# A four-layer graph network: the second layer's update and the output run inside the passes, bucket by bucket

## The reference, cut to what matters

```python
x = x + L0(h)   # edge MLP, summed by dst, then a linear update with a row norm
x = x + L1(h)   # relu(segment_sum(xt[edge_type, dst], src) + bias), xt = h @ weight[r], r = 0..7
x = x + L2(h)   # attention: softmax over the edges of a dst, then a batch norm
x = x + L3(h)   # leaky(segment_sum(w * h[dst], src) @ W + b), w from the degrees by src
```

## Time and profile before

| | us |
|---|---|
| median of 3 runs (5483.92 to 5489.33) | 5488.67 |
| the profiled execution, its own time | 5489.53 |
| its span, first to last instruction | 5487.8 |
| POOL busy | 3830.3 (70%) |
| PE busy | 3680.3 (67%) |
| DVE busy | 3280.8 (60%) |
| ACT busy | 1405.7 (26%) |

### The profile page before, as it was taken

The page is one execution under the profiler, slowest core; times in us unless marked ns, Lnnn a source line. Parts: engine busy times, 40 slices in busy tenths (PEclk is TensorE's granted clock), DMA queues, the critical chain, the costliest instruction groups (busy, mean ns, idle before and its releaser), DMA issues. The chain is left out here.

```text
span 5487.8 us, 118237 instructions
## 1 busy us (share of the span) xinstructions
PE 3680.3 (67%) x13172; PEld 2382.5 (43%) x13177; DVE 3280.8 (60%) x11095; ACT 1405.7 (26%) x4361; POOL 3830.3 (70%) x4005
## 2 busy tenths in 40 slices
PE   5505777777667992666666667777777446676677
PEld 2402443334453441444444456666666324444445
DVE  7315777787643333555555667777777865555556
ACT  0303444444441100000000156655665310000002
POOL 4777777777777776777777537777777257777773
PEclk8755777887788995677777778888888766766768
DMA  2203445444303442445445334444444244445443
GB/s 58 70 26 73 111 111 111 112 111 112 70 3 103 149 144 57 111 112 111 112 111 112 90 92 108 108 108 108 108 109 109 59 112 111 112 111 112 111 111 95
DMA packets 1094230, 543.77 MB, mean 99 GB/s; under 512 B 905511, under 2 KB 991230, under 8 KB 1093881
## 3 DMA queue, kind: packets, MB, share of 16 engines
q0 software_dynamic: 177920, 424.21, 28.0%
q1 hardware_dynamic: 556152, 105.79, 9.7%
q10 hardware_dynamic: 360064, 12.78, 3.6%
HBM read 458.47 MB, written 83.62 MB: 99 GB/s over the span
## 5 line engine op out<-in xcount | busy, mean ns | idle before, releaser
L1311 PE MATMUL psS_plain_src<-got_plain_src,hot_plain_src 128*128 x3328 | 1317.6, 546 | 809.4 <-SPq L1149 562.9
L1311 PEld LDWEIGHTS psS_plain_src<-got_plain_src,hot_plain_src 128*128 128x128 f32 x3328 | 813.8, 266 | 1312.9 <-issue 1189.9
L1194 DVE TENSOR_TENSOR sums<-sums,psS_plain_src 128x257 f32 x1664 | 701.9, 422 | 880.3 <-PE psS_plain_src L1311 718.3
L666 POOL DMA_INDIRECT got_attend_dst<-dram_gtab,recs_attend_dst x832 | 819.6, 985 | 363.3 <-issue 165.6
L542 POOL DMA_INDIRECT dram_rec_src<-rec_src x784 | 766.1, 977 | 289.8 <-issue 241.1
L1166 POOL DMA_INDIRECT got_edge_mlp_dst<-dram_ptab,tile_rec_edge_mlp_dst x784 | 744.3, 949 | 241.8 <-issue 220.1
L1166 POOL DMA_INDIRECT got_plain_src<-dram_htab,tile_rec_plain_src x784 | 743.5, 948 | 242.0 <-issue 219.9
L1166 POOL DMA_INDIRECT got_plain_src<-dram_xtab,tile_rec_plain_src x784 | 743.4, 948 | 241.8 <-issue 214.2
L1322 PE MATMUL psS_edge_mlp_dst<-msg_edge_mlp_dst,hot_edge_mlp_dst 128*128 128x256 f32 x1664 | 653.3, 512 | 151.0 <-DVE sage_sums L1194 123.8
L861 PE MATMUL psS_attend_dst<-msg_attend_dst,hot_attend_dst 128*128 128x264 f32 x1664 | 621.9, 461 | 22.1 <-DVE msg_attend_dst L747 11.9
L1322 PEld LDWEIGHTS psS_edge_mlp_dst<-msg_edge_mlp_dst,hot_edge_mlp_dst 128*128 128x128 f32 x1664 | 344.3, 239 | 290.5 <-DVE sage_sums L1194 105.6
(11 more groups left out here) (347 smaller groups left out, 3957.2 us busy)
## 6 DMA issues: line engine op xcount, KB each, us to landing
dram_xtab<-out_tab SPq DMA_DIRECT2D x48, 1024.0 KB
recs_plain_src<-dram_rec_src ACTq DMA_DIRECT2D x1664, 4.0 KB
tile_rec_plain_src<-dram_rec_src SPq DMA_DIRECT2D x1568, 4.0 KB
recs_edge_mlp_dst<-dram_rec_dst ACTq DMA_DIRECT2D x832, 4.0 KB
recs_attend_dst<-dram_rec_dst SPq DMA_DIRECT2D x832, 4.0 KB
got_attend_dst<-dram_gtab,recs_attend_dst POOLq DMA_INDIRECT x832
dram_rec_src<-rec_src POOLq DMA_INDIRECT x784, 2.1
tile_rec_edge_mlp_dst<-dram_rec_dst SPq DMA_DIRECT2D x784, 4.0 KB
```

The lines of the kernel that those rows point to most:

```text
L666: nc.gpsimd.indirect_dma_start(got[:, u, 0:w], None, table, bass.IndirectOffsetOnAxis(rec_i[:, u, index_word:index_word + 1], 0)).then_inc ...
L1194: nc.vector.tensor_tensor(here, here, psS[t[1] % banks][:, 0:cols], ALU.add).then_inc(added, 1)
L1311: nc.tensor.matmul(psS[t[1] % banks][:, 0:cols], hot[:, t[1], :], flat[:, bass.ds(slots.of(u), cols)], start=True, stop=True).then_inc(sum ...
```

## The change

`run_behind` is a new way to run a ring: from round 5 (`FIRST`) on, after `step(i, u)` it calls `behind(i - 5, u)`. In the two plain passes that is a piece of the work that used to be a stage of its own, on bucket `j = i - 5`, whose sums are complete by then. `RgcnBehind` takes the place of `rgcn_update` and `attention_guard`; `GcnBehind` that of `gcn_output`. Buckets 0 to 46 are done within the rounds, the last two (K = 47 and 48) after the last pair, in `vector_end` and its like, with the range and the guard.

The guard's shift is made from the range alone, with the range in place of the per-node maximum. `c.wide` is kept to the end of the program. It is also set (`c.uneven`) where a bucket `j` of the first 47 has its last pair later than pair `72 + 16 j`, which `PairTables` counts. Where it is set, everything from the pass of L1 on is done again in the old way, on a copy of `x` (`xold`) which SP writes during the pass of L1, one bucket in each round of tiles. `stab` is no longer written on the way that is always taken. The shares in `CUTS` now give 3 rounds of scatters to `place_stage`, then 2, 4, 7, 2, 1 and 10 as before, and 20 to `table_stage` 1.

```diff
-CUTS = 0.04, 0.08, 0.163, 0.306, 0.347, 0.367, 0.57
+CUTS = 0.061, 0.102, 0.184, 0.327, 0.367, 0.388, 0.592
...
+FIRST = 5
...
+    def run_behind(self, eng, step, behind, first, lag):
+
+
+        def a_round(i, more):
+            for u in range(self.size):
+                step(i, u)
+                if more:
+                    behind(i - first, u)
+        a_round(0, False)
+        with eng.Fori(1, first) as i:
+            a_round(i, False)
+        a_round(first, True)
+        with eng.Fori(first + 1, self.rounds - 1) as i:
+            a_round(i, True)
+        a_round(self.rounds - 1, True)
...
+            nc.vector.tensor_tensor(self.late[0:NB, :], self.upto[0:NB, :], c.due[0:NB, :], ALU.is_gt).then_inc(self.lates, 1)
...
+            nc.vector.tensor_scalar(c.uneven[:, :], psX[0:1, 16:17], 0.0, None, ALU.is_gt)
...
+            nc.gpsimd.iota(c.due[:, :], pattern=[[0, 1]], base=U * FIRST - LAG["plain"], channel_multiplier=U,
+                           allow_small_or_imprecise_dtypes=True)
...
+        self.done_by = lambda j: U * (j + FIRST) + 1 - lag
...
+class RgcnBehind(Behind):
+    def keep(self, sp, i):
+        c, rows = self.c, self.c.sh.LAST if isinstance(i, int) and i == self.NB - 1 else P
+        sp.dma_start(c.xold[bass.ds(P * i, rows), :], c.x[0:rows, bass.ds(i, 1), :].rearrange("p a d -> p (a d)")).then_inc(self.kept, 16)
...
+    def vector(self, dve, j, u):
+        nc, c = self.nc, self.c
+        if u == 0:
+            dve.wait_ge(self.added, self.done_by(j))
+            nc.vector.tensor_tensor(self.tmp[:, 0, :], self.row(c.acc, j), c.bias1[:, :], ALU.add).then_inc(self.sums, 1)
+            nc.vector.tensor_copy(self.cnt[:, bass.ds(j, 1)], self.row(c.acc, j, D, D + 1))
+        if u == 1:
+            dve.wait_ge(self.sums, j + 1)
+            dve.wait_ge(self.kept, 16 * (j + 1))
+            x = self.row(c.x, j)
+            nc.vector.scalar_tensor_tensor(x, self.tmp[:, 0, :], 0.0, x, ALU.max, ALU.add).then_inc(self.xs, 1)
+        if u == 2:
+            dve.wait_ge(self.xs, j + 1)
+            self.gate.step()
+            nc.vector.bn_stats(self.stats[:, 0, :], self.row(c.x, j)).then_inc(self.stated, 1)
+            dve.wait_ge(self.stated, 2 * j + 1)
+            self.gate.step()
+            nc.vector.bn_aggr(self.moments[:, 0, :], self.stats[:, 0, :]).then_inc(self.stated, 1)
+            dve.wait_ge(self.stated, 2 * j + 2)
+            nc.vector.tensor_scalar(self.scl[:, 0:1], self.moments[:, 0, 1:2], EPS, None, ALU.add).then_inc(self.begun, 1)
+        if u == 4:
+            dve.wait_ge(self.rooted, j + 1)
+            nc.vector.reciprocal(c.rstd[:, bass.ds(j, 1)], self.scl[:, 0:1]).then_inc(self.scaled, 1)
+            dve.wait_ge(self.scaled, j + 1)
+            nc.vector.scalar_tensor_tensor(c.nbias[:, bass.ds(j, 1)], self.moments[:, 0, 0:1], -1.0, c.rstd[:, bass.ds(j, 1)],
+                                           ALU.mult, ALU.mult).then_inc(self.normed, 1)
+        if u == 15:
+            dve.wait_ge(self.outs, j + 1)
+            self.note(dve, j, 2 * j + 1)
+
+    def note(self, dve, j, zs):
+        nc, c = self.nc, self.c
+        a_src, a_dst = self.row(c.acc, j, D, AW), self.row(c.acc, j, AW, XW)
+        z = self.row(self.z, j, 0, HEADS)
+        dve.wait_ge(self.zs, zs)
+        nc.vector.tensor_tensor(z, a_src, a_dst, ALU.add).then_inc(self.zs, 1)
+        nc.vector.tensor_copy(self.row(c.node, j, 0, HEADS), a_dst)
+        top, low = self.run[:, 0:2 * HEADS], self.run[:, 2 * HEADS:3 * HEADS]
+        nc.vector.tensor_tensor(top, top, self.row(c.acc, j, D, XW), ALU.max)
+        nc.vector.tensor_tensor(low, low, a_src, ALU.min)
+        dve.wait_ge(self.zs, zs + 1)
+        nc.vector.scalar_tensor_tensor(z, z, SLOPE, z, ALU.mult, ALU.max).then_inc(self.zs, 1)
...
+        dve.wait_ge(self.added, self.all)
+        nc.vector.tensor_tensor(self.tmp[:, :, :], c.acc[:, K:NB, 0:D], c.bias1[:, :].unsqueeze(1).to_broadcast([P, 2, D]),
+                                ALU.add).then_inc(self.sums, 1)
...
+        link(all_max(nc, None, dve, self.psR, most, every, 3 * H, self.steps, self.dense, self.diag, c))
+        top = every[:, 0:H].unsqueeze(1).to_broadcast([P, NB, H])
+        nc.vector.tensor_tensor(self.peaks[:, 0, :], every[:, 0:H], every[:, H:2 * H], ALU.add)
+        nc.vector.tensor_copy(self.peaks[:, 1, :], every[:, 0:H])
+        link(nc.vector.tensor_tensor(self.m[:, :, :], c.node[:, 0:NB, 0:H], top, ALU.add))
+        nc.vector.scalar_tensor_tensor(self.peaks[:, :, :], self.peaks[:, :, :], SLOPE, self.peaks[:, :, :], ALU.mult, ALU.max)
+        link(nc.vector.scalar_tensor_tensor(self.m[:, :, :], self.m[:, :, :], SLOPE, self.m[:, :, :], ALU.mult, ALU.max))
+        nc.vector.tensor_tensor(self.z[:, :, :], self.z[:, :, :], self.m[:, :, :], ALU.subtract).then_inc(self.owned, 1)
+        link(nc.vector.tensor_reduce(c.peak[:, :], self.peaks[:, :, :].rearrange("p a h -> p (a h)"), AX.X, ALU.max))
+        nc.vector.tensor_scalar(c.node[:, 0:NB, H:2 * H], self.m[:, :, :], c.peak[:, 0:1], None, ALU.subtract)
+        link(nc.vector.tensor_tensor(self.span[:, :], every[:, 0:H], every[:, 2 * H:3 * H], ALU.add))
+        link(nc.vector.tensor_reduce(self.widest[:, :], self.span[:, :], AX.X, ALU.max))
+        link(nc.vector.tensor_scalar(self.widest[0:1, :], self.widest[0:1, :], SPAN, None, ALU.is_gt))
+        nc.vector.tensor_tensor(c.wide[:, :], self.widest[0:1, :], c.uneven[:, :], ALU.max)
...
+    def scalar(self, act, j, u):
+        nc, c = self.nc, self.c
+        if u == 2:
+            act.wait_ge(self.begun, j + 1)
+            nc.scalar.sqrt(self.scl[:, 0:1], self.scl[:, 0:1]).then_inc(self.rooted, 1)
+        if u == 4:
+            act.wait_ge(self.normed, j + 1)
+            wait_count(act, self.turned, j)
+            nc.scalar.activation(self.h[:, 0, :], self.row(c.x, j), ACT.Relu, bias=c.nbias[:, bass.ds(j, 1)],
+                                 scale=c.rstd[:, bass.ds(j, 1)]).then_inc(self.hs, 1)
+        if u == 6:
+            act.wait_ge(self.turned, j + 1)
+            wait_count(act, self.made, j)
+            nc.scalar.copy(self.hT[:, 0, :], self.psT[:, 0:D]).then_inc(self.hTs, 1)
+        if u == 8:
+            act.wait_ge(self.made, j + 1)
+            nc.scalar.copy(self.row(c.acc, j, 0, XW), self.psO[:, 0:XW]).then_inc(self.outs, 1)
+        if u == 9:
+            act.wait_ge(self.outs, j + 1)
+            act.dma_start(c.gtab[bass.ds(P * j, P), :], self.row(c.acc, j, 0, AW)).then_inc(self.left, 16)
...
+    def tensor(self, pe, j, u):
+        if u == 5:
+            pe.wait_ge(self.hs, j + 1)
+            wait_count(pe, self.hTs, j)
+            self.transposes(self.psT, 0).then_inc(self.turned, 1)
+        if u == 7:
+            pe.wait_ge(self.hTs, j + 1)
+            wait_count(pe, self.outs, j)
+            self.products(self.psO, 0).then_inc(self.made, 1)
...
+class GcnBehind(Behind):
+    def vector(self, dve, j, u):
+        nc, c = self.nc, self.c
+        if u == 12:
+            dve.wait_ge(self.made, j + 1)
+            nc.vector.tensor_tensor(self.y[:, 0, :], self.psO[:, 0:D], c.bias3[:, :], ALU.add).then_inc(self.ys, 1)
+        if u == 13:
+            dve.wait_ge(self.ys, j + 1)
+            wait_count(dve, self.left, 16 * j)
+            nc.vector.scalar_tensor_tensor(self.z[:, 0, :], self.y[:, 0, :], SLOPE, self.y[:, 0, :], ALU.mult, ALU.max).then_inc(self.zs, 1)
+        if u == 14:
+            dve.wait_ge(self.zs, j + 1)
+            nc.vector.tensor_tensor(self.z[:, 0, :], self.z[:, 0, :], self.row(c.x, j), ALU.add).then_inc(self.outs, 1)
...
+    def scalar(self, act, j, u):
+        nc, c = self.nc, self.c
+        if u == 1:
+            act.wait_ge(self.added, self.done_by(j))
+            wait_count(act, self.turned, j)
+            nc.scalar.activation(self.a[:, 0, :], self.row(c.acc, j), ACT.Copy, scale=c.dinv[:, bass.ds(j, 1)]).then_inc(self.scaled, 1)
+        if u == 4:
+            act.wait_ge(self.turned, j + 1)
+            wait_count(act, self.made, j)
+            nc.scalar.copy(self.aT[:, 0, :], self.psT[:, 0:D]).then_inc(self.aTs, 1)
+        if u == 15:
+            act.wait_ge(self.outs, j + 1)
+            act.dma_start(c.out[bass.ds(P * j, P), :], self.z[:, 0, :]).then_inc(self.left, 16)
...
+    def tensor(self, pe, j, u):
+        if u == 3:
+            pe.wait_ge(self.scaled, j + 1)
+            wait_count(pe, self.aTs, j)
+            self.transposes(self.psT, 0).then_inc(self.turned, 1)
+        if u == 5:
+            pe.wait_ge(self.aTs, j + 1)
+            wait_count(pe, self.ys, j)
+            self.products(self.psO, 0).then_inc(self.made, 1)
...
+        after = behind(nc, c, st, nm, pairs, lag, added, psS) if behind else None
...
+                if after is not None and u == 4 and tiles.at(i, u) is not None:
+                    after.keep(sp, i)
...
-            pairs.run(dve, step, lag=lag)
+            if after is None:
+                pairs.run(dve, step, lag=lag)
```

(25 more changed lines are left out.)

284 lines of the change are left out of this document (255 added, 29 removed).

## The result

The changed kernel takes **5411.7 us** (median of 4 runs, 5408.4 to 5414.3), the kernel before, measured with it, 5489.0: a ratio of 0.986, interval 0.985 to 0.987. The forecast was 5355, range 5330 to 5405: the sign was right, the gain is 77 us and not 134, and the time lies 7 us above the range.

A forecast was written before the change was run, and what follows sets the result against it. POOL's gathers were taken to bound each pass, with update, guard and output as gaps between. Terms -80.1 - 56.9 - 5.9 + 2 + 7 = -133.9 us from 5489.5 gave 5355.6, forecast as 5355, range 5330 to 5405.

The forecast's parts named there:

- L1 to L2, -80.1: Between L1's last sums and L2's first gather: 106.0 us of update, branch and guard shrink to a 25.9 us tail, -80.1.
- the hand-over: Between L1's tail and the next pass: switching stages takes 5.8 us, as at this place before.
- The output, -56.9: After L3's last sums: output and end take 17.3 us, including 5.0 for branch and barrier, instead of 74.2: -56.9.
- The scatters, -5.9: One round of 16 scatters moves from `table_stage` 1 (-20.2) to `place_stage` (+14.3): together -5.9 us.
- The work behind at nothing, +2: In 47 rounds of L1 and L3: POOL's gathers hide the added work; only +2 us for the last round.
- the second line of slack: ACT's queue in a round: pair 15's record, fetched behind copies waiting for PE, still fits with 3.6 us to spare.
- The first line of slack: SP's queue: tile records have 3.6 us left, so the copy of `x` fits; at worst +48 us.
- DVE against POOL, +7: In L1 and L3: 118 us of new DVE operations with two SBUF inputs slow POOL's gathers by 6%, +7 us.
- rival A: In the gathers: DVE's two-SBUF-input operations hold POOL for their full length, giving 5466 us; chance 0.04.
- the lesser form of B: Passes of L1 and L3: in-order waits among DVE, ACT and PE lengthen them, time 5405 to 5478 us; chance 0.06.
- C: After L3: the flag is set and everything is done twice, more than 4100 us on top, some 9500; chance 0.01.

The follow-up runs named there:

- experiment 1: Changed kernel with ACT fetching pair records 12 pairs ahead instead of 8 in the plain passes: 5356.3 us, ratio 0.976.
- experiment 4: Kernel with records 12 ahead plus eight unread DVE additions per L1 round: 5369.8 us with both inputs in SBUF, 5356.0 with one in PSUM.
- Experiments 1 and 5: 1: changed kernel, records 12 ahead, 5356.3 us. 5: late-bucket flag instructions removed from that kernel, 5339.9; added to the kernel before, 5502.4; three DVE memsets there instead, 5509.6.
- early12_no_flag: Kernel with records 12 ahead, without the instructions before L0 that find whether a bucket is late: 5339.9 us, ratio 0.973.
- four pads: Kernel with records 12 ahead, late-bucket flag kept, plus four small DVE memsets behind it, ahead of L0: 5349.9 us.

## Why the prediction was wrong

*1. L1 to L2, -80.1.* Measured -84.2 from the last sums on (106.0 to 21.8); the table's row shows -75.0, as the way to the last sums became 9.2 us longer (part 4). Right; the hand-over was over-estimated by 4.3 us.

*2. The output, -56.9.* Measured -58.4 in the span, and -63.7 in the run that has this alone. That run leaves the branch between the passes, which I had costed at 5.0 us, so -61.9 was to be expected of it. Right.

*3. The scatters, -5.9.* Measured -6.2 by the run with this alone, -4.9 by the table's rows. Right.

*4. The work behind at nothing, +2.* **This step failed**: +40.6 in the gathers of L1 and +9.2 in its tail. The new work's operations last the 2.9 us per round that I had added; DVE's busy time grows by less, from 10.0 to 12.2 us of a round of 18.9 and not to 12.9 (514.6 of 800 us from 2300 on in experiment 1), and experiment 4 shows that it had even more room. Wrong was the second line of slack, that between PE's steps 5 and 12 are "7 x 1.18 = 8.3 us" and that "It fits with 3.6 us to spare". The record of pair 15 is needed not when PE comes to pair 12, but when **DVE** begins the places of pairs 12 to 15, at its own step 12; and DVE's step 12 adds the sums of pair 4, since its sums lag by 8. So DVE asks for the record (idle from 2610.77 in the rows above) before PE has even transposed at its step 5 (2611.48), after which ACT fetches it. Of the 4.7 us of transposes, copy, fetch and matrices nothing was covered, and 3.39 us are the wait in the row above. Two engines eight steps apart were put on one time line. With the record fetched 4 pairs earlier the pass is at 984.8 us and its tail, from the last gather to the last sums, at 3.7 in place of 13.9.

The first line of slack, SP's queue with the copies of `x`, held: in experiment 1, with the copies, POOL waits for records hardly longer than before (23.8 us from 2200 to 3100, 22.0 before).

*5. DVE against POOL, +7.* In the kernel of experiment 1 the gathers' busy time, which is free of waits, is 745.7 us in L1 and 745.4 in L3, against 743.4 and 743.5 before: +4.2. Less than the 7, and of its size; the full lock of rival A (+118) is excluded.

*Not in the sum: the pass of L0, +20.1.* I had no term for it, since nothing of it was changed. Without this the changed kernel would be near 5392, inside the range, and without the 50 us of part 4 it would be too: it took both to leave it. Experiments 1 and 5 undo one after the other.

The rivals: what happened is the lesser form of B, 5405 to 5478, to which I gave 0.06. Its tell was named (POOL waiting for records of more than 0.3 us: 2.3 now), but its mechanism was put into DVE's waits for the update's own steps. Those are short in experiment 1 (36.9 us in 900 for the longest of them). C did not happen: no stage follows the pass of L3. With part 4 mended and L0 as before (early12_no_flag, 5339.9 us) the time is 15 us under the forecast and in its range; some 8 of the 15 are the shorter hand-over and the 3.6 us of L2.

The best kernel that keeps all of the change is the one with records 12 ahead: 5356.3 us, ratio 0.976. With four pads it took 5349.9, ratio 0.974 (0.973 to 0.976); the two intervals overlap. Both are faster than the kernel before and the changed one.

## What to carry to other kernels

When work is merged into a loop in which several engines run at a distance from each other, place every wait at the step of the engine that is **ahead**: a prefetch that is issued in order behind such a wait has only the lead that is left there, here 8 steps less 8 of lag. Move the prefetch further ahead first; a queue that doesn't wait would be another way, which was not tried here. And look at the loops that the change doesn't touch: if one of them is as near to its limit as L0 here, a handful of instructions ahead of it can eat a tenth of the gain or more (16 of 148 us here); compare the gathers of every pass, not only of those that were changed.

## What was not expected of the hardware

- The place of a loop in DVE's instruction stream is worth 0.1 to 0.15 us per round, and 7 to 20 us in a pass of 983: three memsets of one element ahead of it made the kernel 15 us slower (5509.6 against 5494.3).
- The tail of L1 in the changed kernel ran near the lower of the clock's two levels, 1.2 GHz: granted 0.54 from 3186 to 3192 us, after PE had waited 5.6 us, where it was 1.00 from 3171 to 3175, amid the pass. The four products took 2.18 us at 3187.48 and 1.08 at 3172.42.
- DVE's additions with one input in PSUM left POOL's issue nearly alone (gathers' mean 955 ns, 951 without it), those with both in SBUF did not (969).
- One chip ran the kernel before in 7506 us in place of 5489; the three kernels with the change that ran there gained 1.8 to 2.0%. Why that chip is slower was not looked into.
